# Operand rows of two small-head attentions: placed by transfers through DRAM, where products with selection matrices and copies out of PSUM placed them

## The reference

```python
q = proj(wq, bq); k = proj(wk, bk); v = proj(wv, bv)     # [heads, T, 8]
q = q * cos + _rotate_half(q) * sin
k = k * cos + _rotate_half(k) * sin
scores = einsum('bhqd,bhkd->bhqk', q, k) * D ** -0.5     # second time: causal
attn = softmax(scores); out = einsum('bhqk,bhkd->bhqd', attn, v)
```

## Time and profile before

| | us |
|---|---|
| median of 3 runs | 2261.64 (2260.36 to 2271.31) |
| the profiled execution | 2265.03 |
| its span (first to last instruction) | 2263.2 |
| first operand stage, start of the span to the next stage's first instruction | 93.76 |
| second operand stage, 1609.3 to 1692.66 | 83.4 |

### The profile page before, as it was taken

The page is one execution under the profiler, slowest core; times in us unless marked ns, Lnnn a source line. Parts: engine busy times, 40 slices in busy tenths (PEclk is TensorE's granted clock), DMA queues, the critical chain, the costliest instruction groups (busy, mean ns, idle before and its releaser), DMA issues. The chain is left out here.

```text
span 2263.2 us, 40233 instructions
## 1 busy us (share of the span) xinstructions
PE 1920.4 (85%) x16064; PEld 932.2 (41%) x16064; DVE 1599.1 (71%) x2303; ACT 1364.7 (60%) x2538; POOL 305.1 (13%) x463
## 2 busy tenths in 40 slices
PE   7769989999999579568888999999586999999675
PEld 2112222222222269534566776777211233334375
DVE  3699999999995343435765777775549988886334
ACT  3239989989989433235544556664342887877321
POOL 2000000000000151413321121111210000000023
PEclk6569999999999779879999999999655999999778
DMA  5000000000000169500000000000100000000075
GB/s 154 1 1 4 6 4 6 4 6 4 6 4 6 40 195 304 165 0 0 1 1 1 1 1 1 1 1 1 48 1 1 5 7 4 7 9 9 12 250 164
DMA packets 51355, 81.34 MB, mean 36 GB/s; under 512 B 7520, under 2 KB 36192, under 8 KB 51040
## 3 DMA queue, kind: packets, MB, share of 16 engines
q1 hardware_dynamic: 46000, 70.30, 9.9%
q0 software_dynamic: 3072, 6.30, 0.9%
q10 hardware_dynamic: 2096, 2.17, 0.3%
HBM read 62.49 MB, written 11.67 MB: 33 GB/s over the span
## 5 line engine op out<-in xcount | busy, mean ns | idle before, releaser
L601 ACT ACTIVATE a0a_probs<-psum 128x512 f32<-128x512 f32 x1024 | 553.8, 596 | 106.2 <-PE psum L541 99.2
L625 DVE TENSOR_REDUCE a0a_mx<-psum 128x2 f32<-128x1024 f32 x512 | 582.9, 1216 | 7.7 <-PE psum L521 7.5
L521 PE MATMUL psum<-a_KS,a_QS 48*128 48x512 bf16 (+3 forms) x1664 | 332.7, 393 | 78.1 <-DVE a0a_mx L625 42.6
L601 ACT ACTIVATE a1a_probs<-psum 128x512 f32<-128x512 f32 (+3 forms) x640 | 304.5, 533 | 117.9 <-PE psum L541 78.4
L625 DVE TENSOR_REDUCE a1a_mx<-psum 128x2 f32<-128x1024 f32 (+2 forms) x320 | 323.8, 1061 | 52.3 <-PE psum L521 29.0
L541 PE MATMUL psum<-a_QS,a_KS 51*128 51x512 bf16 (+3 forms) x1664 | 336.4, 380 | 10.8 <-ACT a1a_probs L601 3.7
L564 PE MATMUL psum<-a0a_probs,a_V 128*16 128x256 f32 x4096 | 325.5, 389 | 8.0 <-ACT a0a_OD L590 5.5
L1589 PE MATMUL psum<-b_VW,b_ST 128*128 128x129 f32 x2176 | 256.6, 280 | 16.2 <-DVE X L1700 16.2
L1589 PEld LDWEIGHTS psum<-b_VW,b_ST 128*128 128x128 f32 x2176 | 253.6, 197 | 17.4 <-DVE X L1700 17.4
L1569 PE MATMUL psum<-b_GT,AT 128*128 128x512 f32 (+3 forms) x640 | 245.3, 537 | 16.9 <-ACT b_ST L1628 16.9
L541 PEld LDWEIGHTS psum<-a_QS,a_KS 51*128 51x128 bf16 x1664 | 87.1, 93 | 367.3 <-ACT a0a_probs L601 195.8
(11 more groups left out here) (221 smaller groups left out, 1776.0 us busy)
## 6 DMA issues: line engine op xcount, KB each, us to landing
e_W<-in_l_experts SPq DMA_DIRECT2D x46, 576.0 KB, 5.2
e_W<-in_l_experts SPq DMA_DIRECT2D x22, 768.0 KB, 6.2
yg<-e_yout SPq DMA_DIRECT2D x14, 256.0 KB, 5.9
xg<-zeros SPq DMA_DIRECT2D x2, 1472.0 KB, 9.4
a_cs<-in_rope ACTq DMA_DIRECT2D x4, 512.0 KB, 9.1
a_cs<-in_rope SPq DMA_DIRECT2D x1, 2048.0 KB, 7.6
e_xin<-xg SPq DMA_DIRECT2D x2, 896.0 KB, 8.0
AT<-in_xT SPq DMA_DIRECT2D x4, 256.0 KB, 6.2
```

The lines of the kernel that those rows point to most:

```text
L521: mm = pe.matmul(ps[:, 2 * slot + half, 0:width], QS[rows, 2 * p + i, q_cols(qb, qt * P, P)], KS[rows, 2 * p + i, c * BLK:c * BLK + width] ...
L601: act.activation(probs[:, e % P_SLOTS, c:BLK], ps[:, S_BANK + e % S_SLOTS, c:BLK], ACT.Exp, scale=scale).then_inc(exp_done, 1)
L625: dve.tensor_reduce(mx[:, pk % 2, qt, 2 * i:2 * i + 2, c], banks, AX.X, ALU.max).then_inc(max_done, 1)
```

## The change

Placing no longer goes over PE and PSUM. A step's three terms are written to a DRAM buffer `kq_terms` (`send`, one transfer for a step: 128 partitions, 3 terms, 512 columns, 384 KB). After every second step `place` waits for the two sends and issues twelve transfers from the DRAM buffer into `KS` or `QS`: for each half (2) and each of the six products, 8 partitions by 8 pairs by 1024 columns, in 64 runs of 2 KB, 128 KB in all. In both stages together these are 16 sends and 96 placing transfers. The rows of -1 come from a tile `minus` by two transfers of 3 partitions. All of them are on SP's queue, ahead of `X` and `later`, and SP ends the stage with a wait for all placed rows. `place`, `kbias`, the selection products, the copies out of PSUM, and the clear and fill of `place` are gone. `t1` and `t2` have three slots and `terms` four; DVE turns two steps ahead, and a term slot is free again when its send has landed. `values` is spread over the first steps.

In the diff, lines of the old functions that stand above in full are left out.

```diff
-        t1, t2 = sb("t1", [P, 2, BLK]), sb("t2", [P, 2, BLK])
-        terms = sb("terms", [P, 2, TERMS, BLK], BF16)
+        t1, t2 = sb("t1", [P, SLOTS, BLK]), sb("t2", [P, SLOTS, BLK])
+        terms = sb("terms", [P, TERM_SLOTS, TERMS, BLK], BF16)
...
+                def send(s):
+                    which, n = steps[s]
+                    sp.wait_ge(low, s + 1)
+                    sp.dma_start(terms_out["kq".index(which)].rearrange("t p c -> p t c")[:, :, block_cols(n)],
+                                 terms[:, s % TERM_SLOTS, :, :]).then_inc(sent[s % TERM_SLOTS], 16)
+                def place(s):
+                    which, n = steps[s]
+                    cols = slice((n - 1) * BLK, (n + 1) * BLK)
+                    for m in (s - 1, s):
+                        sp.wait_ge(sent[m % TERM_SLOTS], 16 * (m // TERM_SLOTS + 1))
+                    for j in range(2):
+                        for r, t in enumerate(K_TERM if which == "k" else Q_TERM):
+                            row = HALF * j + HD * r
+                            heads = terms_out["kq".index(which)][t].rearrange("(u j d) c -> j d u c", j=2, d=HD)
+                            sp.dma_start((KS if which == "k" else QS)[row:row + HD, :, cols], heads[j][:, :, cols]).then_inc(placed, 16)
+                if opening:
+                    opening.sync(sp)
+                sp.wait_ge(minus_set, 1)
+                for j in range(2):
+                    row = HALF * j + SHIFT0
+                    sp.dma_start(KS[row:row + TERMS, :, :], minus[:, :].unsqueeze(1).broadcast_to([TERMS, PAIRS, T])).then_inc(placed, 16)
+                for s in range(NS):
+                    send(s)
+                    if s % 2 == 1:
+                        place(s)
                 if tokens:
-                    opening.sync(sp)
                     sp.dma_start(tokens[0][:, :, :], tokens[1]).then_inc(tokens_in, 16)
                 later(sp)
+                sp.wait_ge(placed, 16 * (2 + 2 * (NS // 2) * len(K_TERM)))
...
-                def place_terms(s):
...
+                project(0)
+                project(1)
+                for s in range(2, NS):
                     project(s)
-                    project_turned(s)
-                for g in range(NB):
-                    values(g)
-                if opening:
-                    opening.placed(pe)
-                for s in range(NS):
-                    place_terms(s)
-            def evacuate(eng, s, v, then):
...
+                    if s - 2 < NB:
+                        values(s - 2)
...
+                def high(s):
+                    u = s % TERM_SLOTS
+                    act.wait_ge(rot, s + 1)
+                    if s >= TERM_SLOTS:
+                        act.wait_ge(sent[u], 16 * (s // TERM_SLOTS))
+                    act.activation(terms[:, u, 0, :], t1[:, s % SLOTS, :], ACT.Copy).then_inc(hi, 1)
...
+                high(0)
+                for s in range(NS):
+                    if s + 1 < NS:
+                        high(s + 1)
+                    middle(s)
...
+                for s in range(NS):
+                    u, k = s % SLOTS, s % TERM_SLOTS
+                    dve.wait_ge(hi, s + 1)
+                    dve.tensor_tensor(t2[:, u, :], t1[:, u, :], terms[:, k, 0, :], ALU.subtract).then_inc(rest, 1)
+                    if s + 2 < NS:
+                        turn(s + 2)
+                    dve.wait_ge(mid, s + 1)
+                    dve.tensor_tensor(terms[:, k, 2, :], t2[:, u, :], terms[:, k, 1, :], ALU.subtract).then_inc(low, 1)
+                    if s < NB:
+                        values(s)
...
-    def gpsimd(self, pool):
...
-    def vector(self, dve):
-        dve.memset(self.place[:, :, :, :, :], 0.0).then_inc(self.blank, 1)
...
+        terms_out = nc.dram_tensor("kq_terms", (2, TERMS, P, T), BF16, kind="Internal").ap()
```

More of the change, by code:

```diff
@@ L94, in settle, with small_head_operands @@
         self.eng.wait_ge(self.sem, self.n)
-def small_head_operands(core, tag, src_T, w, bias, cs, arrived, KS, QS, V, place, kbias, tokens, opening, later):
+def small_head_operands(core, tag, src_T, w, bias, cs, arrived, KS, QS, V, minus, terms_out, tokens, opening, later):
     nc, ps = core.nc, core.psum
+    SLOTS, TERM_SLOTS = 3, 4
     with ExitStack() as st:
@@ L161, in project @@
                         pe.wait_ge(turned, 2 * (s - 1))
-                    pe.matmul(ps[:, 2 * (s % 2), :], w["w" + which][:, :], src_T[:, n * BLK:(n + 1) * BLK], start=True, stop=True)
-                def project_turned(s):
-                    which, n = steps[s]
-                    pe.matmul(ps[:, 2 * (s % 2) + 1, :], w["w" + which + "r"][:, :], src_T[:, n * BLK:(n + 1) * BLK],
+                    cols = src_T[:, block_cols(n)]
+                    pe.matmul(ps[:, 2 * (s % 2), :], w["w" + which][:, :], cols, start=True, stop=True)
+                    pe.matmul(ps[:, 2 * (s % 2) + 1, :], w["w" + which + "r"][:, :], cols,
                               start=True, stop=True).then_inc(qk_ready, 1)
@@ L281, in _ @@
                 if opening:
-                    opening.vector(dve)
                     dve.wait_ge(*arrived["bias"])
                 turn(0)
+                turn(1)
                 dve.wait_ge(ones_set, 1)
-                for g in range(NB):
-                    values(g)
-                for s in range(NS + 1):
-                    if s < NS:
-                        u = s % 2
-                        dve.wait_ge(hi, s + 1)
-                        dve.tensor_tensor(t2[:, u, :], t1[:, u, :], terms[:, u, 0, :], ALU.subtract).then_inc(rest, 1)
-                    if s + 1 < NS:
-                        turn(s + 1)
-                    if s < NS:
-                        dve.wait_ge(mid, s + 1)
-                        dve.tensor_tensor(terms[:, u, 2, :], t2[:, u, :], terms[:, u, 1, :],
-                                          ALU.subtract).then_inc(low, 1)
-                    if s >= 1:
-                        for v in range(BY_ACT, NU):
-                            evacuate(dve, s - 1, v, store)
+                for s in range(NS):
[8 more added lines that the diff above has]
+                        values(s)
                 if opening:
@@ L1856, in scalar @@
             act.dma_start(self.cs[:, :, block(n)], self.a["rope0"][:, :, block(n)]).then_inc(self.cs_in[n], 16)
-    def gpsimd(self, pool):
-        pool.wait_ge(self.ident_in, 16)
-        pool.wait_ge(self.blank, 1)
-        heads = self.core.ident[:, :].rearrange("p (u j d) -> p u j d", u=PAIRS, j=2)
-        for which, terms in enumerate((K_TERM, Q_TERM)):
-            for r, t in enumerate(terms):
-                for j in range(2):
-                    rows = self.place[:, which, t, :, HALF * j + HD * r:HALF * j + HD * (r + 1)]
-                    pool.tensor_copy(rows, heads[:, :, j, :]).then_inc(self.made, 1)
-    def vector(self, dve):
-        dve.memset(self.place[:, :, :, :, :], 0.0).then_inc(self.blank, 1)
     def cast_masks(self, dve):
@@ L1893, in two_layers @@
         AT = sb("AT", [P, T])
-        place = sb("place", [P, 2, TERMS, PAIRS, P], BF16)
-        kbias = sb("kbias", [P, 1])
+        minus = sb("minus", [TERMS, T], BF16)
         columns = sb("columns", [P, len(COLUMNS)])
@@ L1920, in two_layers @@
                     stage = core.sb(st2, "mask_stage", [P, 3, 2, P])
-                    opening = Opening(core, a, place, kbias, AT, w, bias, cs, stage, (columns, a["columns"]), zeros)
+                    opening = Opening(core, a, AT, w, bias, cs, stage, (columns, a["columns"]), zeros)
                     def later(sp):
@@ L1996, in constants @@
         c[name] = np.ascontiguousarray(np.stack([np.tile(cos, (HEADS, 1)), np.tile(sin, (HEADS, 1))], 1), dtype=f)
-    c["kbias"] = np.where((np.arange(P) % HALF >= SHIFT0) & (np.arange(P) % HALF < ROWS), f(-1), f(0)).reshape(P, 1)
     r = np.arange(P) % HALF
```

101 lines of the change are left out of this document (21 added, 80 removed).

## The result

The changed kernel takes 2347.35 us (median of 4 runs, 2343.36 to 2352.03), the kernel before, on the same chip, 2264.78 (4 runs, 2260.36 to 2271.31): a ratio of 1.0363, 95% interval 1.0324 to 1.0401. It is 3.6% slower. The profiled execution took 2343.36 with a span of 2341.6; that of before had a span of 2263.2, so 78.4 us have to be found.

What follows compares the result with a forecast made beforehand. TensorE was taken to bound both operand stages before the change; placing transfers would then set their time. First stage +76 and second +67, together +143 us, gave 2405 us against the median, range 2287 to 2455.

Steps and rivals of the forecast that it cites:

- the likeliest case: Whole program: placing transfers of 2.5 us set the operand stages' time; 2385 to 2440 us, chance 0.70.
- the rival of the engine time: Placing rounds: in a stream each 2 KB run costs 0.175 us, a transfer 1.4 us; 2299 us, chance 0.12.
- the signs: What would show the forecast: operand stages of about 157 and 146 us, rounds near 50 GB/s for 30 us.
- SyncE's waits on `sent`: SyncE's queue: about 24 us of waiting for the sends before the first issue of rounds two to four.
- Terms of steps 0 and 1: First operand stage: VectorE's chain of subtracts and turns completes the first two steps' terms at 23.8 us.
- A placing transfer: Each 128 KB write into eight partitions: priced at 2.5 us, between bounds of 0.8 and 2.8, twelve taking 30 us.
- The burst in the earlier trace: Attention's 16 KB transfers into eight partitions: 47 GB/s over 0.35 us, the evidence for pricing placing transfers.
- the port rule of the Trainium skill: SBUF writes: four neighbouring partitions share a port of about 27 GB/s, so eight reach 54 and a placing takes 2.4 us.
- Turnaround: Between rounds in SyncE's queue: two sends' data, the landing, and issue to data; 4 us.
- Issue: SyncE's queue: 0.67 us for one placing transfer, at least 8 us for twelve, hidden beneath the data.
- Tail: End of the first stage: `X` and `later` still go after the last placing; 9 us, from 4 to 15.
- Full pace: Placing rounds: neighbours don't matter, 0.8 us a transfer; 2241 us, chance 0.14; gain and loss cancel at a 16 us period.

Runs made afterwards that it cites:

- set A: Transfers alone: twelve of the changed kernel's placing transfers, 128 KB each into 8 neighbouring partitions; 65 GB/s, 25.8 us to the next set's first issue.
- m1: Program timing transfers only, not a kernel edit: sets of twelve placing transfers with different partitions, sources or queues; 65 GB/s into 8 neighbours, 166 into rows four apart.
- m2_sharing: Program timing transfers only: sets of eight written repeatedly to the same partitions, then twelve placings alone and behind seven small transfers; four neighbours 26 GB/s, eight 54.
- e8: Changed kernel with the next steps' sends amid the placings in SyncE's queue and product rows six apart; ratio 0.9900 to the kernel before.
- e1: Changed kernel with product rows six apart, so each placing transfer writes 8 partitions six apart; 2263.38 us, ratio 0.9989 to the kernel before.
- e5: Changed kernel with product rows six apart and the sends issued by ScalarE; ratio 0.9865 to the kernel before.
- e7: Changed kernel with the next steps' two sends amid the twelve placings in SyncE's queue, rows kept adjacent; 2250.32 us, ratio 0.9951 to the kernel before.
- m4: Program timing transfers only: 24 adjacent-row placings alone, or with sends of short or long runs from ScalarE's queue or SyncE's own; 31.5 us with the latter.
- set R: Transfers alone: 24 adjacent-row placings with four sends amid them in SyncE's own queue; 31.5 us, 202 GB/s behind the last send.
- e3: Changed kernel with sends issued from ScalarE's queue; 2260.9 us, ratio 1.0001 to before; first-stage placings moved 118 GB/s, not the steady 65 ("the lock").
- m3: Program timing transfers only: 24 adjacent-row placings, alone or beside sends, loads or one small transfer from ScalarE's queue; 44 to 53 us beside these, 50 alone.
- set E: Transfers alone: twelve transfers of 64 KB, each into 4 neighbouring partitions, the next going to other partitions; 75 GB/s.

## Why the prediction was right, and where it was off

Forecast 2405 (range 2287 to 2455), slower with 0.84; measured 2347. The direction and the mechanism held: few partitions written at once set the pace, and rounds in one queue stand behind each other. But 2347 lies below the 2385 to 2440 that was given for the likeliest case, halfway to the rival of the engine time (2299); the wide range, not the likeliest case, holds it. Of the signs, the stages took 131 and 111 us where 157 and 146 were named, and SyncE's waits on `sent` 21.9 where 24 was. By the terms:

- **Terms of steps 0 and 1** at 23.8: the second low term is made at 21.80 + 0.67 = 22.5. The first placing is issued at 25.04, where 26.7 was said.
- **A placing transfer**, 2.5 us: set A of m1 took 57.30 - 31.53 = 25.8 us from its first issue to the next set's, less 1.3 from issue to data and some 0.5 of landing: 24 us for twelve, so 2.0. This is the term that was mis-sized. Over eight rounds it makes most of the error: the first stage was given 4 x 6 = 24 us too much; in the second the four rounds had about 19.6, 23.7, 23.4 and 19 us of data (period less 3.7), together 86 in place of 120, 34 too much. The burst in the earlier trace rows was the right kind of evidence, but it was read too long: the stretch of 0.35 us has idle time at its end (over 0.30 us it is 55 GB/s, as the row below this list has it), and the stretch 190.40:190.60 of the same rows has 72 GB/s. The rest is that in a stream the engines seem not to stay wholly in step: m2_sharing shows 54 GB/s for eight partitions written again and again, and 66 as soon as the next transfer goes elsewhere. With the 2.4 us that the prediction worked out from the port rule of the Trainium skill (an estimate) the forecast would have been some 10 us lower, at about 2395: a better figure for a port, and still too slow for this stream.
- **Turnaround**, 4 us: what is left of the period, 27.7 - 24 = 3.7. Right, as far as a remainder shows it. That it can be had back shows e8 against e1: ratio 0.9900 against 0.9989, some 20 us for six turnarounds.
- **Issue**, 0.67 us: 0.34. It hid beneath the data as said. For rows six apart 0.70 was measured, and there it sets the least that 24 can take (e5).
- **Tail**, 9 us: the fourth round's data ends about 108.13 + 1.3 + 24 = 133.4, and the next stage begins at 142.31: 8.9, barrier included, where 9.9 was said. Right. The issue of `r_wo` waits 20.46 us, but most of that is the round itself.
- **Nothing elsewhere**: the 1519 us between the stages changed by 0.2, the last part by -2.3.

```profile
191.10:191.40 0.30, 0.30 (x8) 0.08 (x8) 0.30 (x1) 0.29 (x2) 0.00 (x0) 1.00 0.29 55
```

Forecast +143, measured +78.4 on the spans: of the difference of 65, 27 lie in the first stage (76 less 48.6), 35 in the second (67 less 31.9), and 2 behind it.

**The rivals.** Full pace (0.8 us a placing, point of decision at a period of 16 us) did not happen in the change, but its pace or nearly so came in e1, e7 and e8: in e1 by the rows alone, in e7 by the order in the queue alone. The prediction named "neighbouring partitions don't matter" as what this rival needs; they matter. Engine time (1.4 us) is no mechanism of its own: the share is 0.52 to 0.54 in the stretches at 65 and at 202 GB/s alike (the change; m4's set R), so a busy engine may be a waiting one. The prediction's reading "each is at share 0.25 only" is off too: the share is a mean over 16 engines, so eight engines at work would stand at 0.5 each in that stretch.

**Open.** Why e3 broke the lock where m3 and m4 with a second queue didn't. The loads of the opening ahead of its placings are not needed: in its second stage the last loads before the placings are issued 38 us ahead of them (1598.16 and 1636.03), and it is faster still (148 GB/s). ScalarE's sends are more and earlier there than in m3 and m4, and this was not tried by itself. That engines are on different transfers when the pace is high is inferred from rates and shares. Why the change's own second stage, with the same queue order, is not held at 65 is open as well (rounds one and four had some 20 us of data). The pace also varies from run to run: the kernels with adjacent rows and broken lock spread over 31 us (e3, nine of ten runs) and 25 us (e7), the change itself over 9, those with rows six apart over 6 to 8 (e1 7, e5 8, e8 6).

## What to carry to other kernels

A transfer into few partitions is priced by which partitions are written at the same time, not by its bytes or by how many DMA engines it has: place rows that belong together four or six apart, as measured here (not 32: those shared a way in), and count who writes at once. A queue that serves a chain of "send, wait, use" should have the next sends amid the uses, not behind them. Work that leaves a compute engine for DMA is only gained if the DMA's stream is shorter than the stage that it joins; work that out from one burst in the trace, in both directions.

## What the runs showed that I had not expected

- At the same share of 0.52 to 0.54 the DMA engines move 65 or, in short stretches, 149 to 202 GB/s into adjacent rows (the change; e7 and m4's set R), depending on what stands between the transfers in their queue.
- Partitions 0, 32, 64 and 96 together take 55 GB/s; 0, 4 ... 28 take 153 (m2_sharing).
- Seven small transfers of one to seven partitions ahead of the twelve raised the pace of their second half to 127 GB/s (m2_sharing).
- Issuing a transfer of 8 x 8 x 1024 costs SyncE 0.34 us into adjacent rows and 0.70 into rows six apart (4.13 and 8.40 us for twelve).
- Four neighbours written in turn with others take 75 GB/s (m1 set E), the same four again and again 26.
